# Weight preparation of a two-layer graph kernel in twenty pieces, each with a place of its own in its engine's order

## The chip, the cores and the metric

The kernel runs on one core of a Trainium2 chip. The metric is the device time of one execution in microseconds. The kernel before takes 776.16 us, the median of three runs (776.13 to 776.79). Engines: TensorE (PE, matmul), VectorE (DVE), ScalarE (ACT), GpSimd (POOL) and SyncE (SP, which here only issues DMAs).

## The reference

64 graphs of 128 nodes and 256 features pass through two layers with a residual each.

```python
h = relu(layernorm(x));  x = x + gat(adj, h)      # two graph-attention layers inside
h = relu(layernorm(x));  x = x + mha(h, adj)      # 8 heads of 32, masked
# gat layer 1 (4 heads of 128): xl = h @ W1; a = <xl, att_src>, b = <xl, att_dst> per head
#   attn = softmax over sources of leaky_relu(a + b), masked; out = elu(attn^T xl + b1)
# gat layer 2 (1 head of 256): the same with W2, att_src2, att_dst2, b2, without elu
# mha: softmax(q k^T / sqrt(32)) v, relu, @ Wo
```

## The kernel before, in words

One graph fills the 128 partitions, so the kernel is a loop over 64 graphs. A graph passes through some fifty small functions on five engines. They are software-pipelined: in step t an engine calls each of its functions for graph t minus a lag that stands beside the function in a list (`(gat1_exp, 4)`), in the order of the list. `run` calls a function only while its graph exists; 75 steps in all. Engines synchronise by one semaphore per function; `done` waits for the producer of the same graph, `free` for the reader of the buffer two graphs back, and `after` and `at_ends` (only the first and last 12 graphs) for readers of a PSUM bank that several results share. An engine runs its list strictly in order.

Graph g's way: `norm1_moments`, `variance1` (VectorE), `rsqrt1` (GpSimd), `norm1_apply`, `relu1` (ScalarE), `relu1_low` (VectorE; h is kept as two halves of 16 bits), `norm1_transpose` (a DMA issued by SyncE gives hT), `project1` (TensorE), `ab_high`, `ab_low`, `xl_evac` (VectorE), `transpose_ab`, `abT_copy`, `scores1_mask` and `scores1`, `gat1_leaky`, `gat1_scores` (row maximum), `gat1_exp`, `gat1_recip`, `normalise` (GpSimd), `transpose1`, `gat1_copy` (en), `aggregate1`, `elu_exp` (ScalarE), `elu` (VectorE, h1T), `project2`, `ab2_evac`, `diagonal2`, `scores2`, `gat2_leaky`, `gat2_scores`, `gat2_exp`, `transpose2`, `gat2_copy`, `aggregate2`, `residual1`; the second norm in the same way to h2T; `qk`, `qk_copy`, `qk_low`, `scores3_mask`, `scores3_first`, `scores3_last`, `mha_max` (VectorE: top3, nmx3), `mha_exp_first` and `mha_exp_last` (four exponentials each), `e3_first_halves` and `e3_last_halves` (GpSimd), `e3_transpose_first` and `_last` (DMA), `project_v`, `mha_av`, `att_norm`, `att_copy`, `att_low`, `att_transpose` (DMA), `project_out`, `residual2`, `store`.

Ahead of this the weights are prepared. W1 gets four columns more (`prod`, then sums over each head); its largest element and that of the columns are found, turned and spread over the partitions by TensorE, rounded to powers of two, and the scaled W1 is split into two 16-bit halves. The four projection matrices get the same treatment in one go (`proj_split`: ScalarE's `split_high`, GpSimd's `split_low`). W2 gets two columns from `prod2`, and a product of W2 with ones gives a correction for b2 and for the scores (`shift2`). Before, this stands in blocks that are called in front of a whole step (`before={3: ..., 4: ...}`): VectorE's `prepare_w1`, `prepare_b1` ahead of step 3, `prepare_w2` ahead of step 4; GpSimd's `products_w1` and `picks` ahead of step 3, `products_w2` ahead of 4; TensorE's `spread_largest` ahead of steps 0 and 4; and `w2_sums` inside `project2` and `ab2_evac` of graph 0. SyncE issues x of two graphs, then W1, att1, b1, x, adj, W2, att2, b2 and the projections.

## Time and profile before

| | |
|---|---|
| median of three runs | 776.16 us |
| the profiled execution | 774.69 us |
| its span, first to last instruction | 772.6 us |
| TensorE busy | 716.3 us (93%) |
| VectorE busy | 681.4 us (88%) |
| ScalarE busy | 591.6 us (77%) |
| GpSimd busy | 515.8 us (67%) |

The rows further down come from one profiled execution. Times are us from its first instruction. A window row gives a stretch and its length, then the busy time and, in brackets, the number of instructions of PE, PEld (TensorE's weight loads), DVE, ACT and POOL, the granted TensorE clock, the busy share of the DMA engines and GB/s. A timeline row gives start, duration and the operation with output <- input; "xN" are N instructions merged. Matmul ends are modelled, and consecutive matmuls overlap, so the distance between starts says more than a duration. 32-bit products take two instructions each in the trace.

### The profile page before, as it was taken

How to read it: one execution, taken by the hardware profiler on the slowest of the kernel's cores; microseconds unless marked ns; L12 is line 12 of the kernel's file. 1: busy time of each engine (PE TensorE's matmuls, PEld its weight loads, DVE VectorE, ACT ScalarE, POOL GpSimd, SP SyncE). 2: the span in 40 equal slices, each digit the busy share in tenths (PEclk: the TensorE clock that was granted, in tenths of full speed). 3: DMA queues.
4: the chain of work that ended last, by engine and by line, in shares of the span. 5: the costliest groups of instructions: out<-in, count | busy, mean ns of one | idle time of the engine just before them, and what ended most of it. 6: DMA issues, size and time to landing. Idle time of an engine off the chain costs nothing.

```text
span 772.6 us, 26496 instructions
## 1 busy us (share of the span) xinstructions
PE 716.3 (93%) x8398; PEld 593.4 (77%) x8398; DVE 681.4 (88%) x2017; ACT 591.6 (77%) x1865; POOL 515.8 (67%) x733
## 2 busy tenths in 40 slices
PE   0389999999999999999999999999999999999973
PEld 0157788888888888888888888888888888788852
DVE  4758899999999999999999999999999989999873
ACT  0167888888888778888888788788888888788752
POOL 5456777676767676667667766676677767766551
PEclk9999999999999999999999999999999999999996
DMA  6111555666578566557766656766655666655464
GB/s 197 33 37 43 106 112 112 121 110 118 118 117 115 116 112 113 119 114 115 122 110 118 112 124 115 115 110 120 114 119 116 113 119 106 112 118 105 89 110 89
DMA packets 270423, 84.70 MB, mean 110 GB/s; under 512 B 242896, under 2 KB 269904, under 8 KB 270288
## 3 DMA queue, kind: packets, MB, share of 16 engines
q1 hardware_dynamic: 270288, 83.02, 57.8%
q8 instruction: 70, 1.15, 0.7%
q14 instruction: 65, 0.53, 0.3%
HBM read 15.86 MB, written 8.39 MB: 31 GB/s over the span
## 4 chain that ended last, share of the span: by engine, by line
PE 75%; DVE 9%; DMA 5%; issue 4%; SPq 3%; ACT 1%; POOL 1%; DVEq 0%; ACTq 0%; POOLq 0%
PE bank L815 28%; PE bank L840 11%; PE bank L986 7%; PE bank L947 6%; DMA hT<-h_split 4%; PE bank L966 3%; PE bank L929 3%; PE bank L936 3%; PE bank L866 3%; PE bank L891 2%; PE bank L889 2%; PE bank L881 2%; SPq L276 1%; DVE top L756 1%; PE bank L874 1%
## 5 line engine op out<-in xcount | busy, mean ns | idle before, releaser
L497 ACT ACTIVATE e<-bank,nmx,q_power 128x128 f32<-128x128 f32 x512 | 194.7, 481 | 5.1 <-DVE nmx L761 5.1
L372 POOL CAST e_split<-e 128x512 f16<-128x512 f32 x128 | 82.4, 643 | 118.6 <-ACT e L497 118.6
L374 POOL TENSOR_TENSOR e_split<-e,e_split 128x512 f16<-128x512 f32 x128 | 151.7, 1185 | 10.3
L840 PE MATMUL bank<-w,h1T 128*128 128x258 f32 x512 | 122.8, 382 | 0.7 <-DVE shift L599 0.7
L386 POOL TENSOR_TENSOR rstd<-var,minus_half 128x1 f32<-128x1 f32 x128 | 71.7, 560 | 66.6 <-DVE var L625 66.6
L815 PE MATMUL bank<-w_split,hT 128*128 128x260 f16 x768 | 98.2, 278 | 12.3 <-DMA hT<-h_split 11.9
L840 PEld LDWEIGHTS bank<-w,h1T 128*128 128x128 f32 x512 | 96.6, 190 | 16.6 <-DVE h1T L655 1.6
L448 ACT ACTIVATE eT<-lr,nmx 128x128 f32<-128x128 f32 x256 | 102.7, 458 | 0.8 <-DVE nmx L713 0.8
L815 PE MATMUL bank<-h2T,proj_split 128*128 128x128 f16 x1536 | 97.4, 220 | 1.6 <-DMA h2T<-h_split 1.6
L815 PEld LDWEIGHTS bank<-h2T,proj_split 128*128 128x128 f16 x1536 | 92.0, 99 | 3.7 <-DMA h2T<-h_split 2.4
L815 PEld LDWEIGHTS bank<-w_split,hT 128*128 128x128 f16 x768 | 71.1, 98 | 24.5 <-issue 7.0
L364 POOL TENSOR_TENSOR eTn<-eT,rs 128x512 f32<-128x512 f32 x64 | 67.0, 1046 | 17.9 <-DVE rs L752 17.9
L756 DVE TENSOR_REDUCE top<-bank 128x8 f32<-128x1024 f32 x64 | 77.3, 1208 | 0.3 <-PE bank L947 0.3
L424 ACT ACTIVATE h_split<-z 128x256 f16<-128x256 f32 x64 | 26.6, 416 | 65.9 <-DVE z L631 65.9
L947 PEld LDWEIGHTS bank<-qkT 32*128 32x128 f16 x1536 | 43.0, 93 | 37.7 <-issue 36.0
L986 PE MATMUL bank<-en,xl 128*128 128x128 f32 x512 | 68.3, 276 | 0.2
L448 ACT ACTIVATION_READ_ACCUMULATOR eT<-lr,nmx 128x1 f32 x256 | 65.7, 257 | 0.0
L947 PE MATMUL bank<-qkT 32*128 32x128 f16 x1536 | 64.8, 216 | 0.3 <-DVE qkT L724 0.2
L986 PEld LDWEIGHTS bank<-en,xl 128*128 128x128 f32 x512 | 62.2, 192 | 2.0 <-ACT en L455 1.3
L604 DVE SCALAR_TENSOR_TENSOR h_split<-z,h_split 128x256 f16<-128x256 f32 x128 | 61.5, 481 | 0.6 <-ACT h_split L424 0.5
L815 PE MATMUL bank<-proj_split,attT 128*128 128x256 f16 x384 | 54.3, 279 | 6.1 <-DMA attT<-att_split 6.1
L440 ACT ACTIVATE lr<-bank,ab 128x128 f32<-128x128 f32 x64 | 23.5, 368 | 43.6 <-PE bank L867 43.6
(116 smaller groups left out, 1921.7 us busy)
## 6 DMA issues: line engine op xcount, KB each, us to landing
x_in<-in_x_dram SPq DMA_DIRECT2D x64, 128.0 KB, 2.3
out_dram<-x_out SPq DMA_DIRECT2D x64, 128.0 KB, 2.0
adj_in<-in_adj_dram SPq DMA_DIRECT2D x64, 64.0 KB, 2.5
e3T<-e_split SPq DMA_TRANSPOSE x128, 3.1
hT<-h_split SPq DMA_TRANSPOSE x64, 2.4
h2T<-h_split SPq DMA_TRANSPOSE x64, 2.5
attT<-att_split SPq DMA_TRANSPOSE x64, 2.8
w<-in_L_gnn_W_dram SPq DMA_DIRECT2D x2, 256.0 KB, 3.1
```

What stands on the lines that cost most here:

```text
L364: pool.tensor_tensor(eTn[:, g.two, :].rearrange("p (h n) -> p h n", h=H), eT[:, g.two, :].rearrange("p (h n) -> p h n", h=H), rs[:, g.two, ...
L372: pool.tensor_copy(e3_split[:, g.two, half, 0], e).then_inc(s[high_set], 1)
L374: pool.tensor_tensor(e3_split[:, g.two, half, 1], e, e3_split[:, g.two, half, 0], ALU.subtract).then_inc(s[low_set], 1)
L386: pool.tensor_tensor(rstd[:, g.two, which:which + 1], var[:, g.two, which:which + 1], minus_half[:, :], ALU.pow).then_inc(s[rstd_set], 1)
L448: ins = act.activation(eT[:, g.two, h * N:(h + 1) * N], lr[:, g.two, h * N:(h + 1) * N], ACT.Exp, bias=nmx[:, g.two, h:h + 1], accum_out=s ...
L497: ins = act.activation(e3[:, g.two, h, :], S[:, h // 4, (h % 4) * N:(h % 4 + 1) * N], ACT.Exp, bias=nmx3[:, g.two, h:h + 1], scale=q_power ...
L604: dve.scalar_tensor_tensor(out=out_, in0=in_, scalar=0.0, in1=high_, op0=ALU.max, op1=ALU.subtract).then_inc(s[sem_], 1)
L756: dve.tensor_reduce(top3[:, g.two, :], S.rearrange("p b (h n) -> p (b h) n", h=4), AX.X, ALU.max, negate=True).then_inc(s["top3_set"], 1)
L815: ins = pe.matmul(out_, left, right, start=n == 0, stop=n == len(pairs) - 1)
L840: ins = pe.matmul(X2[:, 0:D + 2], h1T[:, g.two, k * F:(k + 1) * F], w2[:, k, :], start=k == 0, stop=k == H - 1)
L947: ins = pe.matmul(S[:, b, col * N:(col + 1) * N], qkT[r, g.two, i, h // 4, :], qkT[r, g.two, j, 2 + h // 4, :], start=False, stop=n == 2 a ...
L986: ins = pe.matmul(O1[:, h * N:(h + 1) * N], xl[:, g.two, h * F:(h + 1) * F], en[:, g.two, h * N:(h + 1) * N], start=True, stop=True)
```

## The change

Every piece of the preparation becomes a function of its own with a lag in the list of its engine (`@once`: it runs for graph 0 only). The orders and lags of all five engines are written anew, and with them the PSUM banks of the results and the waits `after` and `at_ends`; the arithmetic is the same. A new wait `after_once` guards banks that preparation and loop share. The weights' semaphores are divided (`w1_in`, `att1_in`, `b1_in`; a set of its own for w1 and for proj in place of the counted `power_set` and the like). ScalarE issues the loads of att1 and b1; SyncE issues W1 first.

```diff
-        XL = bank[:, 0:2, :]   ABT = bank[:, 2, ...]   Z = 3   ET = 6   O1 = 1   X2 = 6   Z2 = 7
-        ET2 = 6   O2 = 2   QK = 7   V = 3   S = 4:6   AV = 2   WO = 0
+        XL = bank[:, 6:8, :]   ABT = bank[:, 6, ...]   Z = 2   ET = 0   O1 = 3   X2 = 3   Z2 = 2
+        ET2 = 7   O2 = 6   QK = 7   V = 1   S = 4:6   AV = 0   WO = 0
+        W2_SUMS = bank[:, 4]
+        PREP = {"w1": bank[:, 2], "proj": bank[:, 4]}
...
+def after_once(eng, sem, g, lag, value=1):
+    if 0 <= g.n + lag and g.n < LAGS:
+        eng.wait_ge(sem, value)
...
+        def once(function):
+            def first(g):
+                if g.n == 0:
+                    function(g)
+            return first
...
 SyncE
-            for n in range(2):
-                sp.dma_start(x_in[:, n, :], x[n]).then_inc(x_here[n], 16)
             for k in range(KD):
                 sp.dma_start(w1[:, k, :, 0:HF // 2], ...).then_inc(s["w1_in"], 16)
-            for k in range(2):
-                sp.dma_start(att1[:, k, :], ...).then_inc(s["w1_in"], 16)
-            sp.dma_start(b1_all[:, :], ...).then_inc(s["w1_in"], 16)
-            sp.dma_start(x_in[:, 2, :], x[2]).then_inc(x_here[2], 16)
+            for n in range(3):
+                sp.dma_start(x_in[:, n, :], x[n]).then_inc(x_here[n], 16)
...
-                (e3_transpose_last, 9), (att_transpose, 10), (store, 11), (norm1_transpose, 3), (e3_transpose_first, 8),
-                (load_adj, 1), (load_x, 0), (norm2_transpose, 6),
+                (load_x, 0), (load_adj, 1), (store, 11), (norm1_transpose, 3), (e3_transpose_last, 8), (norm2_transpose, 6),
+                (e3_transpose_first, 8), (att_transpose, 9),
 GpSimd
-                (e3_last_halves, 9), (masks, 3), (e3_first_halves, 8), (rsqrt1, 2), (rsqrt2, 6), (diagonal2, 5),
-                (normalise, 4),
-            before={3: (products_w1(), picks()), 4: products_w2, 5: (split_low(0), split_low(1)), 6: split_low(2), 7: split_low(3)}
+                (products_w2, 4), (e3_first_halves, 11), (e3_last_halves, 10), (split_low3, 11), (rsqrt1, 3), (rsqrt2, 8),
+                (diagonal2, 7), (split_low2, 9), (picks, 1), (products_w1, 1), (normalise, 6), (split_low0, 8),
+                (split_low1, 8), (masks, 3),
 ScalarE
+            for k in range(2):
+                act.dma_start(att1[:, k, :], ...).then_inc(s["att1_in"], 16)
+            act.dma_start(b1_all[:, :], b1.partition_broadcast(128)).then_inc(s["b1_in"], 16)
...
-                (v_copy, 9), (relu1, 3), (gat2_leaky, 6), (att_copy, 10), (abT_copy, 4), (gat1_copy, 5), (gat2_exp, 6),
-                (gat1_leaky, 4), (mha_exp_first, 8), (elu_exp, 5), (gat2_copy, 6), (mha_exp_last, 8), (qk_copy, 7),
-                (gat1_exp, 4), (relu2, 6),
-            before={5: (split_high(0), split_high(1)), 6: split_high(2), 7: split_high(3)}
+                (split_high3, 9), (gat2_exp, 7), (gat1_copy, 6), (att_copy, 11), (v_copy, 9), (gat2_copy, 7), (abT_copy, 5),
+                (mha_exp_last, 9), (elu_exp, 6), (split_high2, 8), (gat1_leaky, 5), (mha_exp_first, 9), (split_high0, 7),
+                (qk_copy, 8), (gat1_exp, 5), (relu1, 3), (relu2, 7), (gat2_leaky, 6), (split_high1, 7),
 VectorE
-                (xl2_evac, 6), (relu2_low, 7), (ab_high, 4), (v_low, 9), (ab_low, 4), (xl_evac, 4), (gat2_scores, 6),
-                (mha_max, 8), (att_low, 10), (relu1_low, 3), (residual2, 11), (norm1_moments, 2), (gat1_scores, 4), (elu, 5),
-                (gat2_recip, 6), (variance1, 2), (residual1, 6), (norm2_moments, 6), (variance2, 6), (qk_low, 7),
-                (ab2_evac, 5), (norm2_apply, 6), (gat1_recip, 4), (att_norm, 9), (norm1_apply, 2),
-            before={3: (prepare_w1(), prepare_b1()), 4: prepare_w2}
+                (w1_largest, 0), (variance2, 7), (v_low, 9), (qk_low, 8), (b1_prep, 4), (ab2_evac, 6), (xl2_evac, 6),
+                (norm2_apply, 7), (proj_row, 6), (w1_sums, 2), (gat1_recip, 5), (norm1_moments, 1), (relu1_low, 3),
+                (att_norm, 10), (relu2_low, 7), (gat2_scores, 6), (ab_high, 4), (xl_evac, 4), (w1_scale, 3), (w1_products, 0),
+                (ab_low, 4), (proj_scale, 6), (w1_row, 2), (mha_max, 8), (gat2_recip, 6), (att_low, 10), (proj_largest, 5),
+                (residual2, 11), (variance1, 1), (residual1, 6), (elu, 5), (norm2_moments, 6), (w2_sums, 4), (w2_shift, 5),
+                (gat1_scores, 4), (norm1_apply, 2),
 TensorE
+            @once
+            def w2_ones(g):
+                pe.wait_ge(s["w2_set"], 2)
+                pe.wait_ge(s["ones_set"], 4)
+                at_ends(pe, s["e3_first"], g, -3)
+                after_once(pe, power_set["proj"], g, -1)
+                for k in range(H):
+                    ins = pe.matmul(W2_SUMS[:, 0:D + 2], ones[:, :], w2[:, k, :], start=k == 0, stop=k == H - 1)
+                ins.then_inc(s["w2_summed"], 1)
...
-                (scores3_mask, 8), (scores3_first, 8), (scores2, 6), (scores3_last, 8), (transpose_ab, 4), (transpose1, 5),
-                (scores1_mask, 4), (scores1, 4), (project_out, 11), (aggregate1, 5), (transpose2, 6), (project_v, 8), (qk, 7),
-                (aggregate2, 6), (project2, 5), (mha_av, 9), (project1, 3),
-            before={0: spread_largest(0, 0, 2, 2), 4: spread_largest(1, 2, 6, 3)}
+                (turn_w1, 0), (spread_w1, 0), (project1, 0), (scores3_last, 4), (transpose1, 1), (project_v, 4),
+                (scores1_mask, 0), (transpose2, 2), (transpose_ab, 0), (project_out, 7), (aggregate1, 1), (aggregate2, 2),
+                (scores1, 0), (qk, 3), (project2, 1), (scores3_mask, 3), (mha_av, 5), (scores3_first, 3), (turn_proj, 1),
+                (scores2, 1), (w2_ones, 0), (spread_proj, 1),
```

## Rows read from the trace of the kernel before

**Rows 1.** Page: busy time of each engine, and the chain by engine.

```profile
PE 716.3 (93%) x8398; PEld 593.4 (77%) x8398; DVE 681.4 (88%) x2017; ACT 591.6 (77%) x1865; POOL 515.8 (67%) x733
...
PE 75%; DVE 9%; DMA 5%; issue 4%; SPq 3%; ACT 1%; POOL 1%; DVEq 0%; ACTq 0%; POOLq 0%
```

**Rows 2.** Windows: busy us (instructions) of each engine, granted clock, DMA.

```profile
0.00:40.00 40.00, 8.63 (x37) 5.12 (x37) 22.64 (x53) 5.55 (x15) 18.40 (x35) 1.00 0.39 111
140.00:640.00 500.00, 496.88 (x5961) 416.93 (x5961) 468.87 (x1411) 415.08 (x1319) 353.29 (x502) 1.00 0.65 116
718.00:773.00 55.00, 38.25 (x483) 29.02 (x481) 32.24 (x81) 28.39 (x84) 21.46 (x27) 0.84 0.52 99
```

**Rows 3.** Timeline of TensorE, `scores1_mask` of six graphs: start, us, what.

```profile
34.31 0.63 PE L881 MATMUL bank<-ident,mask_gat 128*128 128x512 f16 x1
...
61.34 0.38 PE L881 MATMUL bank<-ident,mask_gat 128*128 128x512 f16 x1
...
113.24 0.38 PE L881 MATMUL bank<-ident,mask_gat 128*128 128x512 f16 x1
...
354.97 0.38 PE L881 MATMUL bank<-ident,mask_gat 128*128 128x512 f16 x1
...
365.83 0.38 PE L881 MATMUL bank<-ident,mask_gat 128*128 128x512 f16 x1
...
718.26 0.38 PE L881 MATMUL bank<-ident,mask_gat 128*128 128x512 f16 x1
```

**Rows 4.** Timeline of the head: start, us, what, [idle before, releaser].

```profile
11.06 1.22 DVE L552 TENSOR_REDUCE largest<-w 128x1 f32<-128x1024 f32 x1 [6.18 <-DMA b_all<-in_L_gnn_b_dram]
...
20.83 1.69 DVE L571 SCALAR_TENSOR_TENSOR w_split<-w,scale,w_split 128x512 f16<-128x512 f32 x4
...
24.68 4.64 POOL L345 TENSOR_TENSOR prod<-w,att 128x512 f32<-128x512 f32 x4
...
26.00 2.76 PE L815 MATMUL bank<-w_split,hT 128*128 128x260 f16 x12 [6.99 <-DMA hT<-h_split]
...
45.28 2.01 PE L802 MATMUL bank<-w,ones 128*128 128x258 f32 x8 [1.50 <-DVE h1T L655]
```

**Rows 5.** Timeline of one step in the loop, ScalarE, then VectorE.

```profile
411.46 1.51 ACT L497 ACTIVATE e<-bank,nmx,q_power 128x128 f32<-128x128 f32 x4
...
412.85 0.70 ACT L460 ACTIVATE ex<-bank,minus_one 128x512 f32<-128x512 f32 x1
...
409.86 1.21 DVE L756 TENSOR_REDUCE top<-bank 128x8 f32<-128x1024 f32 x1
...
413.88 0.68 DVE L655 SCALAR_TENSOR_TENSOR h1T<-ex,bank 128x512 f32<-128x512 f32 x1
```

**Rows 6.** Groups of instructions from 200 to 600 us: busy us, mean ns.

```profile
L738 DVE SCALAR_TENSOR_TENSOR x<-bank,rs,x_in 128x256 f32<-128x256 f32 x36 | 17.4, 484 | 12.8 <-PE bank L929 12.8
...
L773 DVE SCALAR_TENSOR_TENSOR x_out<-bank,out_power,x 128x256 f32<-128x256 f32 x37 | 17.4, 472 | 0.0
```

**Rows 7.** The line that applies a norm: duration ns min/median/max.

```profile
L631 DVE TENSOR_SCALAR z<-x_in,mv,rstd x64: 376/798/1256, 4.5 to 704.7; 128x256 f32<-128x256 f32 x64
```

**Rows 8.** SyncE's issue of one hT, its use, the landing of all 64.

```profile
600.24 1.19 SPq L263 DMA_TRANSPOSE hT<-h_split  x1
...
603.41 1.49 PE L815 MATMUL bank<-w_split,hT 128*128 128x260 f16 x12
...
DMA to landing us min/median/max: 2.4/2.4/4.2
```

**Rows 9.** Waits: who waited for whom, us in total, times, longest.

```profile
PE bank L815 <- DMA hT<-h_split: 11.9, 9, 7.0
...
DVE h1T L655 <- ACT ex L460: 8.8, 19, 1.4
```

**Rows 10.** Timeline of the tail: `transpose2` and `qk` of graph 63.

```profile
738.17 0.33 PE L912 MATMUL bank<-ident,eT 128*128 128x128 f32 x1 [0.78 <-ACT eT L471]
...
748.20 2.03 PE L815 MATMUL bank<-h2T,proj_split 128*128 128x128 f16 x18 [1.25 <-DMA h2T<-h_split]
```

More of the change, by code:

```diff
@@ L203, in gnn_kernel @@
         s = {n: sem(n) for n in names}
+        turned = {n: sem(f"turned_{n}") for n in ("w1", "proj")}
+        row_set = {n: sem(f"row_set_{n}") for n in turned}
+        diag_set = {n: sem(f"diag_set_{n}") for n in turned}
+        spread = {n: sem(f"spread_{n}") for n in turned}
+        power_set = {n: sem(f"power_set_{n}") for n in turned}
+        scale_set = {n: sem(f"scale_set_{n}") for n in turned}
         x_here = [sem(f"x_here{i}") for i in range(8)]
@@ L351, in split_low, with split_low0, split_low1, split_low2 @@
                 pool.tensor_tensor(proj_split[:, 1, :, m, :], proj[:, :, m, :], proj_split[:, 0, :, m, :], ALU.subtract).then_inc(s["split_low"], 1)
+            @once
+            def split_low0(g):
+                split_low(0)
+            @once
+            def split_low1(g):
+                split_low(1)
+            @once
+            def split_low2(g):
+                split_low(2)
+            @once
+            def split_low3(g):
+                split_low(3)
             def diagonal2(g):
@@ L549, in prepare_w1, with rows_of_largest @@
-            def prepare_w1():
-                dve.wait_ge(s["w1_in"], 16 * 5)
-                dve.wait_ge(s["ident_set"], 5)
-                dve.tensor_reduce(largest[:, 0:1], w1[:, :, :, high], AX.XYZ, ALU.max, apply_absolute_value=True).then_inc(s["largest_set"], 1)
+            def rows_of_largest(n, first, last):
+                rows, column = last - first, list(turned).index(n)
+                dve.wait_ge(turned[n], 1)
+                dve.tensor_reduce(row_largest[0:rows, column:column + 1], PREP[n][0:rows, 0:128], AX.X, ALU.max).then_inc(row_set[n], 1)
+                dve.wait_ge(row_set[n], 1)
+                dve.tensor_scalar(largest_diag[0:rows, first:last], ident[0:rows, 0:rows], row_largest[0:rows, column:column + 1], None,
+                                  ALU.mult).then_inc(diag_set[n], 1)
@@ L553, in prepare_w1, with w1_largest, w1_products @@
+            @once
+            def w1_largest(g):
+                dve.wait_ge(s["w1_in"], 16 * KD)
+                dve.tensor_reduce(largest[:, 0:1], w1[:, :, :, high], AX.XYZ, ALU.max, apply_absolute_value=True).then_inc(s["largest_w1"], 1)
+            @once
+            def w1_products(g):
+                dve.wait_ge(s["w1_in"], 16 * KD)
+                dve.wait_ge(s["att1_in"], 16 * 2)
                 for k in range(KD):
@@ L785, in _, with turn_w1 @@
         @block.tensor
         def _(pe):
-            def spread_largest(n, first, last, count):
+            @once
+            def turn_w1(g):
                 pe.wait_ge(s["ident_set"], 5)
-                pe.wait_ge(s["ones_set"], 4)
-                pe.wait_ge(s["largest_set"], count)
-                rows = last - first
-                pe.transpose(S[0:rows, n, 0:128], largest[:, first:last], ident[:, :]).then_inc(s["largest_turned"], 1)
-                pe.wait_ge(s["largest_diag_set"], n + 1)
-                pe.matmul(S[:, n, 128:128 + rows], ones[0:rows, :], largest_diag[0:rows, first:last], start=True, stop=True).then_inc(s["largest_spread"], 1)
-                pe.wait_ge(s["power_set"], 2 * n + 1)
@@ L798, in w2_sums, with spread_w1 @@
-            def w2_sums():
+                pe.wait_ge(s["largest_w1"], 2)
+                at_ends(pe, s["lr_set"], g, -1)
+                at_ends(pe, s["lr2_set"], g, -2)
+                pe.transpose(PREP["w1"][0:2, 0:128], largest[:, 0:2], ident[:, :]).then_inc(turned["w1"], 1)
+            @once
+            def spread_w1(g):
+                pe.wait_ge(s["ones_set"], 4)
+                pe.wait_ge(diag_set["w1"], 1)
+                pe.matmul(PREP["w1"][:, 128:130], ones[0:2, :], largest_diag[0:2, 0:2], start=True, stop=True).then_inc(spread["w1"], 1)
@@ new lines, in turn_proj, with spread_proj @@
+            @once
+            def turn_proj(g):
+                pe.wait_ge(s["ident_set"], 5)
+                pe.wait_ge(s["largest_proj"], 1)
+                at_ends(pe, s["e3_first"], g, -2)
+                after_once(pe, s["shift2_set"], g, 0, 2)
+                pe.transpose(PREP["proj"][0:4, 0:128], largest[:, 2:6], ident[:, :]).then_inc(turned["proj"], 1)
+            @once
+            def spread_proj(g):
+                pe.wait_ge(s["ones_set"], 4)
+                pe.wait_ge(diag_set["proj"], 1)
+                pe.matmul(PREP["proj"][:, 128:132], ones[0:4, :], largest_diag[0:4, 2:6], start=True, stop=True).then_inc(spread["proj"], 1)
@@ L799, in w2_sums @@
+            @once
+            def w2_ones(g):
                 pe.wait_ge(s["w2_set"], 2)
                 pe.wait_ge(s["ones_set"], 4)
+                at_ends(pe, s["e3_first"], g, -3)
+                after_once(pe, power_set["proj"], g, -1)
                 for k in range(H):
-                    ins = pe.matmul(X2[:, 0:D + 2], ones[:, :], w2[:, k, :], start=k == 0, stop=k == H - 1)
+                    ins = pe.matmul(W2_SUMS[:, 0:D + 2], ones[:, :], w2[:, k, :], start=k == 0, stop=k == H - 1)
```

193 lines of the change are left out of this document (113 added, 80 removed).

## The prediction

> **What bounds the kernel now.** I read the page's busy times first, then the windows, then the marks of one TensorE instruction per graph, and only then single stretches. The reader is to see that TensorE is busy 93% of the span and that three quarters of the chain that ended last lie on it [rows 1]; that in the middle it is busy 496.88 of 500 us, against 8.63 of the first 40 and 38.25 of the last 55 [rows 2]. So the middle is TensorE's own work, and what can be won cheaply lies in the first 40 us and in the last 55.
>
> The mask product of the first attention (`scores1_mask`) runs once per graph and is my clock for the loop [rows 3]: graph 0 at 34.31, graph 3 at 61.34, graph 8 at 113.24, graph 63 at 718.26. Two neighbours without a disturbance lie 10.86 apart (365.83 - 354.97). From graph 8 to 63 there are 55 steps in 605.0 us, 11.0 each: 55 x 10.86 = 597.3 is TensorE without a gap, 7.7 us are stalls. Three stretches follow: head (to 113.2), loop (605.0) and tail (718.26 to 772.6, 54.3).
>
> **Head.** What the block at the start costs now [rows 4]: VectorE waits until 11.06 for the transfer of b1, the fifth that the first weight semaphore counts; its block runs to 20.83 + 1.69 = 22.5, that is 11.4 us; the first `project1` starts at 26.00, after the halves of h have been made behind the block and turned by DMA. Then the scores of graph 0 and `project1(1)` wait behind the second block, which itself waits for GpSimd's four products (24.68 to 29.3); the first score mask comes only at 34.31 [rows 3]. The sum over W2 on TensorE (2.01 us at 45.28) and its evacuation stand directly ahead of `project2(0)`.
>
> After the change W1 is the first transfer, att1 and b1 are issued by ScalarE, and b1 is waited for only in its own piece. The gate of the W1 products is then att1's landing. The bounds are 4.9 (where VectorE fell idle, 11.06 - 6.18) and 11.06; two loads of x no longer stand ahead and b1 is no longer counted, but W1 and att1 are 1 MB that still have to come, so I take 8.0. The rest of the W1 block is 11.4 - 1.2 (the maximum, done while att1 lands) = 10.2 us, and between its pieces now stand three moments of x, one norm and one remainder, some 2.3 us by the loop's durations: the W1 pieces end at 20.5. hT is issued some 3 us before that and takes 2.4 to land [rows 8], so it is covered. `project1(0)` starts at 20.5, 5.5 earlier.
> Rule against it, which none of these numbers uses: the Trainium skill, DMA: Bandwidth & Descriptors, section Issuing engines are not separate DMA queues, says that transfers from any engine share the same DMA engines and that a second issuer saves only issue time. By that ScalarE's three issues save some 1.5 us and the rest must come from the order; the sum would be about 2 us later. No row of this kernel shows loads issued by ScalarE.
>
> From there I followed graph 0 by the durations of the trace. xl is done at 23.2 (2.76 us for the product [rows 4]), ab_split 24.3, scores 26.0, leaky 26.8; VectorE does the W2 sums (2.4 us) just in that wait, so they are nearly free; row maximum 27.5, exponentials 29.2. `w2_ones` takes 2.0 us of TensorE ahead of `project1(1)`; it ends near 28.9, `project1(1)` near 31.5, mask of graph 1 at 32. `proj_largest` (2.3 us) falls into the wait for graph 0's transpose, normalised copy and aggregation, so `project2(0)` starts near 35.8 (now some 48, behind the W2 sums). Then: mask of graph 2 near 41, of graph 3 near 50 (now 61.34). Here the price of the split pieces falls due: eight ScalarE copies of 512 elements (0.7 us as `elu_exp` [rows 5]) and four GpSimd subtractions (1.2 us, a quarter of its four products) sit in steps in which graphs 1 to 3 already run; I give them 1.2 us in all, graph 4 at 60.7. Then TensorE is full: 9.6 + 10.2 + 10.2 + 10.9 (the step without, with `mha_av`, with `project_out`) and 0.8 for stalls puts graph 8 at 102.4. Head: 113.2 - 102.4 = **10.8 us won**. Bounds: 13 (dense from graph 3 on) and 5 (the split pieces and the W2 pieces each hold a whole step up, as the second block does now).
>
> **Loop.** The instructions are the same, but the diff rewrites every engine's order, the PSUM banks and the waits between engines; so "no change" has to be shown. I laid the new orders out against TensorE's dense 10.86 us, with zero at `project1`. TensorE's hand-overs fit: ab_split is ready at 2.4, wanted at 3.1; en at 3.0, wanted by `project_out` at 3.25 (its bank is ET's); h1T at 6.8, wanted at 7.1; diag2 at 9.7, wanted at 10.4; the score bank free at 7.8, wanted at 8.8. Two circles are tight.
> Circle one goes `mha_max` -> four exponentials -> `elu_exp` -> `elu` -> VectorE's order -> next `mha_max`. ScalarE's part is 1.4 us to the start of `elu_exp` (411.46 to 412.85) + 0.70 + hand-overs, 2.2 in all [rows 5]. In the order of before five pieces of VectorE fill that gap; now it holds att_low, two residuals [rows 6] and two ops of 0.15, 1.3 us by issue spacing. So VectorE idles 0.9 us there. Its busy time is 468.87 / 500 x 11.0 = 10.31 us a step [rows 2], and 10.31 + 0.9 = 11.2 would be over 10.86. But of this 10.31 the norm of x takes 0.80 (median; shortest 0.38 [rows 7]), with GpSimd at work beside it; in the new order it falls where GpSimd has finished the late halves and waits for variance2. With 0.4 instead of 0.8, and 0.2 of overlap of the small ops' tails (issued 0.07 to 0.09 apart, 0.15 long), the circle is 10.6 to 10.8: just under TensorE.
> Circle two goes over SyncE. In the order of before hT is issued at 600.24 and used at 603.41 [rows 8], 3.2 us on; it lands in 2.4 (up to 4.2), and hT's lateness makes 4.9 of the 7.7 us of stalls (11.9 less the 7.0 of the first [rows 9]). Now `store` and `norm1_transpose` stand behind `e3_transpose_first` and `att_transpose` and two loads. By my layout e3_transpose_first is issued at 4.3, and 1.25 + 1.25 + 0.5 + 0.6 + 0.6 us of issues later hT at 8.5, for a use at 10.86: 2.36 us for a landing of 2.4. That circle spans two steps and gives 10.95 us a step, and it has no room for a slow landing. 55 x 10.95 = 602.3 and 1.7 for slow ones: 604, **1 us won**. Both ends: 597.3 (-7.7) and 11.15 a step, 613 (+8).
>
> **Tail.** After graph 63's mask the rest of a graph's chain runs alone. Now `transpose2(63)` is at 738.17, and `qk(63)` at 748.20 [rows 10], 10.0 us on; in the new order `aggregate2` stands ahead of `qk(62)`, not behind it (1.5 us), and `transpose2(63)` comes some 0.8 us earlier from the mask. The rest (two e3 transposes, `mha_av`, out, store) keeps its length. **2.3 us won**, bounds 0 and 4.
>
> **Sum.** The profiled execution took 774.69 (span 772.6 and 2.1 around it). 774.69 - 10.8 - 1.0 - 2.3 = 760.6. The median of the runs is 776.16, 1.5 above the profiled one: 762.
>
> **Rivals.** A, the loop gets denser: hT lands in time after all and both circles stay under 10.86: 762 - 6 = 756. For it: GpSimd's late halves could be earlier than I placed them; against it the 2.36 us.
> B, VectorE becomes the bound through circle one: the norm keeps 0.80 because GpSimd works beside it. 11.1 us a step, 55 x 0.15 = 8 us over my 10.95: 770. For it: `elu` already waited 19 times, 8.8 us, for `elu_exp` [rows 9]. Beside this, the Trainium skill, SBUF — State Buffer, section Who interferes with whom: a VectorE operation in a two-port mode and GpSimd lock each other out for a whole instruction; the 376 to 1256 ns of one shape [rows 7] agree that it can be long, though the median is twice the shortest and not a whole GpSimd instruction of 1.2 us more.
> C, the pieces hold the first graphs up: head won only 5 us: 768.
> D, slower than before: SyncE's queue sets the loop. If the issue of hT comes 0.6 us later than placed (att_low behind GpSimd's halves, a store that waits for `project_out`) the two-step circle is 22.5 us, 11.25 a step, 55 x 0.3 = 16 us over my loop: 778. It decides against the change from 0.27 us a step over 10.95 on, where 55 x 0.27 eats the 14 us.
> E, a loop stall that cancels the head: 775 to 778.
>
> **How the numbers follow.** Chances: forecast 0.52, A 0.14, B 0.14, C 0.08, D 0.09, E 0.03. The forecast with A, B and C makes faster, 0.88, less a little for B and C falling together: 0.85. No change (within 0.2%, 1.6 us, about what a measurement tells) is E and the edge of D: 0.04. Slower: 0.11. The range has the low end at 762 less the rest of A and 2 us of head (753), the high end at B with 5 us of C (775).
>
> **What would show it.** Right: masks of graph 0 near 24, graph 3 near 50, graph 8 near 102; `project2(0)` near 36; norm of x (L631's line) well under 0.8; VectorE idle at `elu` in most steps but TensorE without gaps; hT issued 2.3 to 2.5 us before `project1`. Wrong: att1 landing after 9.5; mask distances over 11.1 in the middle; a wait of TensorE for h1T or hT in every step (B or D); a gap over 2 us at `qk(0)` or `project_v(0)` for the split weights (C).

## The result, and the profile after

The changed kernel takes 812.42 us (median of 4 runs, 809.96 to 817.27) against 776.14 us (775.66 to 776.79), a ratio of 1.0475, interval 1.0423 to 1.0526. It is 36 us slower; the forecast was 762 us, and even rival D, the one on the slower side, gave 778.

The profiled execution took 817.27 us, its span is 814.8; it is the slowest of the four, so stretches read from it are some 5 us longer in sum than the median's. I read it in the order in which the prediction was made. First the page, busy times and the chain by engine, which answers to [rows 1]:

```profile
PE 729.6 (90%) x8398; PEld 598.9 (74%) x8398; DVE 682.6 (84%) x2017; ACT 586.8 (72%) x1865; POOL 532.0 (65%) x733
...
ACT 23%; issue 18%; DVE 13%; PE 13%; DMA 11%; SPq 11%; POOL 10%; POOLq 0%; ACTq 0%; DVEq 0%
```

The reader is to see the second line. No engine's busy time has grown by more than 17 us, but the chain that ended last has left TensorE: 75% of it was there, now 13%, and the rest wanders over every engine and over SyncE's queue (SPq). That is what a kernel looks like that is bound by a circle of waits and not by an engine. The windows, columns as in [rows 2]:

```profile
0.00:40.00 40.00, 13.97 (x64) 9.46 (x65) 26.30 (x61) 7.17 (x18) 24.54 (x43) 1.00 0.45 125
140.00:640.00 500.00, 473.34 (x5528) 392.93 (x5526) 434.49 (x1311) 382.12 (x1227) 339.74 (x465) 0.99 0.61 108
762.00:815.00 53.00, 36.35 (x477) 27.63 (x474) 32.06 (x80) 28.16 (x82) 21.15 (x26) 0.85 0.55 101
```

The head is fuller (13.97 us of TensorE in 40, not 8.63), the middle has lost what made it dense: 473.34 of 500 and not 496.88. `scores1_mask` (L997 now), to be laid beside [rows 3]:

```profile
26.27 0.63 PE L997 MATMUL bank<-ident,mask_gat 128*128 128x512 f16 x1
...
54.07 0.38 PE L997 MATMUL bank<-ident,mask_gat 128*128 128x512 f16 x1
...
113.38 0.38 PE L997 MATMUL bank<-ident,mask_gat 128*128 128x512 f16 x1
...
762.07 0.38 PE L997 MATMUL bank<-ident,mask_gat 128*128 128x512 f16 x1
```

| stretch | before | predicted | after |
|---|---|---|---|
| head, to the mask of graph 8 | 113.2 | 102.4 | 113.4 |
| loop, graph 8 to 63 | 605.0 (11.00 a step) | 604 (10.95) | 648.7 (11.79) |
| tail | 54.3 | 52.0 | 52.7 |

The whole loss is the loop's 43.7 us. The head's gain was there (8.0 us at graph 0, 7.3 at graph 3) and was given back by graph 8. A part of that is the new, slower loop, in which those five steps already run: e11, below, has the loop mended and takes 56.0 us from graph 3 to graph 8, against 59.3 here and 51.9 before. In the waits (who waited for whom, us in total, times, longest) two things that hardly showed before now lead at TensorE:

```profile
PE bank L927 <- DMA hT<-h_split: 28.7, 24, 2.3
...
DVE h1T L748 <- ACT ex L517: 24.7, 37, 1.5
...
PE bank L953 <- DVE h1T L748: 10.4, 26, 1.1
```

Inside the loop (marks 8 to 63) they make 27.0 us for hT (23 times) and 6.0 for h1T (20 times), against 3.3 for hT before. That is 29.7 of the 43.7. The rest is busy time: 473.34/500 x 11.79 is 11.16 us of TensorE a step against 10.93 before, 12.6 us over 55 steps. Some 3.2 of them are three `project1` that ran wholly or partly at the lower clock (2.78, 2.78 and 2.10 us instead of 1.49, see below). That the others are matmuls that start after a gap and so don't overlap with a neighbour (42 gaps in the middle 500 us, 11 before) is my reading and not shown.

The chain of waits between 301 and 325 us says why hT is late; start, us, what:

```profile
305.94 1.44 ACT eT L505 x7
...
308.93 0.71 POOL absent L437
...
309.72 0.95 POOL mask_mha L438
...
310.73 0.46 POOL mask_gat L440
311.19 0.56 POOL e_split L408
...
311.83 1.17 POOL e_split L410
...
313.01 1.23 SPq L278
...
314.34 1.25 SPq L297
...
315.64 0.57 SPq L263
...
316.26 0.42 SPq L269
316.73 0.43 SPq L273
...
317.25 4.63 DMA hT<-h_split
...
321.93 2.78 PE bank L927 x12
```

This is circle two of the prediction with its full length. GpSimd makes the masks (2.3 us with their gaps, 308.93 to 311.19) and only then the halves of e3; SyncE issues the turn of e3 (L278), then that of att (L297), two loads and the store, and hT last: 317.25, some 4.2 us behind the e3 issue, though h was ready long before (in a later step its remainder is made at 416.39 and the turn issued at 425.32). `project1` starts the next round through the queues: `transpose1` stands behind it on TensorE (L1085, from 325.23), ScalarE's `gat1_copy` waits for that near the head of its list, and the exponentials of the mha and of the first attention stand behind `gat1_copy` and feed the same GpSimd queue. The wait of `gat1_copy`, over the whole kernel:

```profile
ACT en L512 <- PE bank L1085: 41.5, 32, 3.5
```

From `ex` at 303.07 to `ex` two steps on, at 328.65, the same chain takes 25.6 us; 2.2 of it are a slow landing (4.63 instead of the median 2.4). Without it, 23.4/2 = 11.7 a step. This slow landing costs twice: TensorE had stood for 2.0 us, and its 12 matmuls took 2.78 us and not 1.49. The window of just that product shows the lower of the two clock levels, 0.50 (1.2 GHz):

```profile
321.90:324.70 2.80, 2.77 (x14) 1.71 (x16) 0.00 (x0) 0.46 (x2) 2.42 (x4) 0.50 0.31 61
```

One more view, a step on VectorE and GpSimd side by side (timeline, columns as in [rows 5]). It is where the second surprise lies:

```profile
416.39 0.93 DVE L697 SCALAR_TENSOR_TENSOR h_split<-z,h_split 128x256 f16<-128x256 f32 x1
...
417.82 0.42 DVE L697 SCALAR_TENSOR_TENSOR h_split<-z,h_split 128x256 f16<-128x256 f32 x1
...
420.40 0.70 DVE L852 TENSOR_SCALAR nmx<-top,q_power 128x8 f32<-128x8 f32 x1
```

```profile
416.00 1.04 POOL L400 TENSOR_TENSOR eTn<-eT,rs 128x512 f32<-128x512 f32 x1 [0.54 <-DVE rs L843]
...
417.80 0.95 POOL L438 TENSOR_SCALAR mask_mha<-adj_in 128x128 bf16<-128x128 int32 x1
...
419.91 1.16 POOL L410 TENSOR_TENSOR e_split<-e,e_split 128x512 f16<-128x512 f32 x1
```

The two remainders have one line and one shape. That of h, `relu1_low`, starts inside GpSimd's `normalise` and takes 0.93 us; that of h2, `relu2_low`, takes 0.42, though GpSimd is at work there too, on `mask_mha`, and it is `mask_mha` that takes 0.95 where it took 0.66 elsewhere. The scaling of nmx3, 8 columns, takes 0.70 when it meets the subtraction of the halves, and ends 0.03 us behind it (421.10, 421.07); in the step before, with GpSimd idle, it took 0.23 (409.22). By this the Trainium skill, SBUF — State Buffer, section Who interferes with whom, is borne out in kind: VectorE and GpSimd share a pair of ports and lock each other out.

### The profile page after: what moved, and what is told of

Read it like the earlier page. It is cut to its first block, busy times and chain, and to the rows that moved or that the text cites. A ratio compares the mean times of both kernels' runs of the same rounds, so it can differ in the third digit from the quotient of the medians.

```text
span 814.8 us, 26593 instructions
## 1 busy us (share of the span) xinstructions
PE 729.6 (90%) x8398; PEld 598.9 (74%) x8398; DVE 682.6 (84%) x2017; ACT 586.8 (72%) x1865; POOL 532.0 (65%) x733
## 4 chain that ended last, share of the span: by engine, by line
ACT 23%; issue 18%; DVE 13%; PE 13%; DMA 11%; SPq 11%; POOL 10%; POOLq 0%; ACTq 0%; DVEq 0%
ACT e L554 11%; DMA hT<-h_split 9%; ACT eT L505 7%; PE bank L927 6%; SPq L297 4%; SPq L278 3%; POOL e_split L410 3%; DVE top L847 3%; ACT ex L517 2%; POOL mask_mha L438 2%; POOL absent L437 2%; PE bank L1085 2%; DVE nmx L852 2%; SPq L263 2%; POOL e_split L408 2%
## 5 line engine op out<-in xcount | busy, mean ns | idle before, releaser
L408 POOL CAST e_split<-e 128x512 f16<-128x512 f32 x128 | 78.9, 616 | 133.7 <-ACT e L554 133.7
L953 PE MATMUL bank<-w,h1T 128*128 128x258 f32 x512 | 126.3, 389 | 11.0 <-DVE h1T L748 10.4
L953 PEld LDWEIGHTS bank<-w,h1T 128*128 128x128 f32 x512 | 92.1, 190 | 26.8 <-DVE h1T L748 15.6
L505 ACT ACTIVATE eT<-lr,nmx 128x128 f32<-128x128 f32 x256 | 101.5, 438 | 2.3 <-DVE nmx L804 2.3
L528 ACT ACTIVATE eT<-lr,nmx 128x128 f32<-128x128 f32 x64 | 25.7, 402 | 92.0 <-DVE nmx L796 92.0
L927 PEld LDWEIGHTS bank<-h2T,proj_split 128*128 128x128 f16 x1536 | 88.2, 98 | 3.4 <-DMA h2T<-h_split 3.3
L697 DVE SCALAR_TENSOR_TENSOR h_split<-z,h_split 128x256 f16<-128x256 f32 x128 | 90.4, 708 | 0.3
L512 ACT ACTIVATE en<-bank 128x512 f32<-128x512 f32 x64 | 38.1, 595 | 42.9 <-PE bank L1085 41.5
L748 DVE SCALAR_TENSOR_TENSOR h1T<-ex,bank 128x512 f32<-128x512 f32 x64 | 44.0, 687 | 25.3 <-ACT ex L517 24.7
L505 ACT ACTIVATION_READ_ACCUMULATOR eT<-lr,nmx 128x1 f32 x256 | 60.6, 237 | 0.0
L438 POOL TENSOR_SCALAR mask_mha<-adj_in 128x128 bf16<-128x128 int32 x64 | 55.3, 864 | 5.1
```

Of the source, the lines that this page charges most:

```text
L408: pool.tensor_copy(e3_split[:, g.two, half, 0], e).then_inc(s[high_set], 1)
L438: pool.tensor_scalar(mask_mha[:, g.eight, :], adj_in[:, g.four, :], 0.0, -BIG, ALU.is_equal, ALU.mult)
L505: ins = act.activation(eT[:, g.two, h * N:(h + 1) * N], lr[:, g.two, h * N:(h + 1) * N], ACT.Exp, bias=nmx[:, g.two, h:h + 1], accum_out=s ...
L697: dve.scalar_tensor_tensor(out=out_, in0=in_, scalar=0.0, in1=high_, op0=ALU.max, op1=ALU.subtract).then_inc(s[sem_], 1)
L927: ins = pe.matmul(out_, left, right, start=n == 0, stop=n == len(pairs) - 1)
L953: ins = pe.matmul(X2[:, 0:D + 2], h1T[:, g.two, k * F:(k + 1) * F], w2[:, k, :], start=k == 0, stop=k == H - 1)
```

## Experiments

Two theories stood at the start. **SyncE's queue** (rival D, circle two): hT waits behind e3, att, loads and store. **VectorE and ScalarE** (circle one): from the row maximum `mha_max` over ScalarE's exponentials and back through VectorE's order. Each edit is against the changed kernel unless said otherwise; "step" is the loop's us per graph between the marks of graphs 8 and 63, read from one execution. The kernel before was measured again beside each group of runs (medians 776.14, 773.74, 772.65 and 773.15 us), so kernels of different groups are compared by their ratios.

| kernel | us | ratio to before, 95% | step |
|---|---|---|---|
| changed kernel | 812.42 | 1.0475 (1.0423 to 1.0526) | 11.79 |
| e1, hT ahead on SyncE | 792.02 | 1.0223 (1.018 to 1.0266) | 11.38 |
| e2, moments moved | 819.88 | 1.0586 (1.0538 to 1.0635) | 11.80 |
| e3, both | 794.58 | 1.0265 (1.0226 to 1.0304) | 11.36 |
| e5, pieces in the old loop | 769.77 | 0.9957 (0.9935 to 0.9979) | 11.01 |
| e4, masks between the halves | 780.17 | 1.0093 (1.0066 to 1.012) | 11.18 |
| e6, other places | 787.96 | 1.0194 (1.015 to 1.0238) | 11.33 |
| e7, `elu_exp` first | 819.60 | 1.06 (1.055 to 1.0651) | 11.87 |
| e9, W2 pieces later | 774.31 | 0.9998 (0.9969 to 1.0026) | 11.03 |
| e10 = e4 + e1 | 770.66 | 0.9966 (0.995 to 0.9981) | 11.03 |
| e11 = e10 + a swap | 767.08 | 0.9916 (0.9884 to 0.9947) | 10.96 |

**e1, hT ahead on SyncE.** The turn of h is issued one step earlier, behind the last half of e3, and no longer at the end of the queue.

```diff
 SyncE
-    (load_x, 0), (load_adj, 1), (store, 11), (norm1_transpose, 3), (e3_transpose_last, 8), (norm2_transpose, 6),
+    (load_x, 0), (load_adj, 1), (store, 11), (e3_transpose_last, 8), (norm1_transpose, 2), (norm2_transpose, 6),
```

> The changed kernel with one edit on SyncE: norm1_transpose stands ahead of norm2_transpose with lag 2 instead of behind store with lag 3, so hT is issued some 8 us ahead of its use. In the changed kernel the loop from graph 8 to 63 took 648.7 us (11.8 a step); project1 waited for hT 28.7 us in 24 of its steps, and project2 for h1T 10.4 us. Theory 1 (a circle over two steps, project1 -> VectorE -> GpSimd's normalise, masks and first halves -> SyncE's queue -> hT -> project1, sets the loop; the circle mha_max -> exponentials -> elu_exp -> elu comes second): no wait for hT is left, the second circle then gives about 11.3 a step, loop 620, total 784. Theory 2 (the circle through elu sets the loop, the wait for hT only follows from it): the waits move to h1T, loop stays above 640, total 805 or more. Theory 3 (either alone explains all): loop 600, total 764.

Measured: 20 us faster than the changed kernel; every wait for hT is gone (in the loop `project1` now starts 10.2 to 10.9 us after the issue), and the step is 11.38. Theory 1 had 11.3 and 784 us: the right case, 8 us too low. What is left is the other circle:

```profile
DVE h1T L748 <- ACT ex L517: 41.5, 59, 1.5
...
PE bank L953 <- DVE h1T L748: 15.2, 36, 1.1
```

So SyncE's queue sets the step at 11.79, and a second circle lies close below it, at 11.38. Taking the first away gives only half of the loss back.

**e2 and e3, the moments of x moved.** `norm1_moments` goes out of the crowded part of VectorE's order into the gap in which `elu` waits: alone (e2), and with e1's edit (e3).

```diff
 VectorE
-    (gat1_recip, 5), (norm1_moments, 1), (relu1_low, 3),
+    (gat1_recip, 5), (relu1_low, 3),
...
-    (residual2, 11), (variance1, 1), (residual1, 6), (elu, 5),
+    (residual2, 11), (norm1_moments, 1), (variance1, 1), (residual1, 6), (elu, 5),
```

> The changed kernel with one edit on VectorE: norm1_moments moves from behind gat1_recip to just ahead of variance1, that is into the gap between mha_max and elu, where VectorE waits for ScalarE. That takes 0.55 us out of the circle mha_max -> exponentials -> elu_exp -> elu and nothing out of the circle over SyncE. Theory 1: the wait for hT stays, the loop gains 0 to 0.2 us a step, total 801 to 812. Theory 2: 0.5 us a step, total 785.

> Both edits together. Theory 1: both circles come near TensorE's own 10.9 us: 10.9 to 11.1 a step, loop 600 to 610, total 765 to 775, and more is gained than by the two edits singly. Theory 2: as the second edit alone, 785. A third theory (VectorE's longer remainders and nmx3 beside GpSimd are a cost in themselves, whatever the circles): above 780, with VectorE busy over 95%.

Measured: e2 gained nothing in the loop (11.80), as it must while SyncE's queue sets the step. In all it is even slower than the changed kernel (1.0586 against 1.0475, the intervals apart) and above both of its expectations; why is open, since the two profiled executions differ by 1.1 us only. But e3 gained nothing over e1 either (11.36 against 11.38), and 0.6 us had been taken out of what I held to be the circle. Its time lies with the third theory, above 780, but VectorE is busy 90% and not over 95%, so none of the three was met. The chain of e3 between two row maxima shows both what the circle really is and where the 0.6 us went:

```profile
407.51 1.14 DVE top L847
...
408.68 0.71 DVE nmx L852
...
410.92 0.11 ACT ex L517
...
411.37 0.71 ACT lr L490
412.08 0.63 ACT e L554 x2
...
413.79 1.69 ACT eT L505 x8
415.48 0.32 ACT h_split L481
...
415.82 0.07 DVE h_split L697
415.89 1.13 issue
417.02 0.21 DVE rs L785
...
419.00 1.14 DVE top L847
```

The circle doesn't return through `elu`. It goes on along ScalarE's queue, over leaky, the other four exponentials (`mha_exp_first`) and the four of the first attention (`eT`, 413.79), and enters VectorE again behind them: 11.49 us from maximum to maximum. In e1 it takes the same way, except that it enters VectorE at `norm1_moments`, which stands behind `gat1_recip` and its wait for `eT`; between 200 and 600 us the chain of e1 passes `mha_max` 34 times and `elu` once. And the 0.6 us are eaten at one place. With the moments gone the remainder starts together with GpSimd's `normalise` and takes 1.27 us, not 0.93; ahead of it VectorE waits for ScalarE's relu. In e1 and in e3 `rs` (L785) starts at the same 417.02. Over the whole kernel the mean of the two remainders is 871 ns in e3 and 859 in e2, against 708 in the changed kernel and 481 before.

**e5, the pieces in the old loop.** The kernel before, with its own lists, banks and lags, and only the preparation cut up and the load order changed. ScalarE's split copies, GpSimd's products and subtractions and the first W1 pieces of VectorE and TensorE still stand in blocks ahead of whole steps; in the changed kernel all 27 pieces (not twenty, as the title has it) have places of their own.

```diff
 SyncE: W1 first; att1 and b1 issued by ScalarE
 GpSimd
+    before={2: products_w1, 3: picks, 4: products_w2, 6: (split_low(0), split_low(1)), 7: split_low(2), 8: split_low(3)}
 ScalarE
+    before={6: (split_high(0), split_high(1)), 7: split_high(2), 8: split_high(3)}
 VectorE (once each, for graph 0; the other entries as before)
+    before={2: (w1_largest, w1_products), 3: w1_sums}
+    (b1_prep, 4), (w2_sums, 4), (w1_row, 3), (w1_scale, 3), (proj_largest, 4), (w2_shift, 5), (proj_row, 5), (proj_scale, 5),
 TensorE
+    before={0: (turn_w1, spread_w1)}
+    (w2_ones, 4) behind scores1; turn_proj, spread_proj (5) behind project2
```

> The kernel before with its loop orders, lags and banks kept as they are, and only the preparation cut into pieces between the first graphs (and W1 loaded first, att1 and b1 issued by ScalarE). If the head is worth what the changed kernel's head showed at graph 0 to 3 (marks 8.0 and 7.2 us earlier), and the loss is all in the loop, this gives 766 to 769. If the pieces cost as much in the first eight steps as they give, as the changed kernel's mark of graph 8 (113.4 against 113.2) could also be read, it stays at 775 to 777.

Measured: 4 us faster than before, between the two cases (the first meant 7 to 10), and the loop is the old one (11.01). So this cutting up is worth 0.4%, and the 36 us are all in the rewritten orders with their lags and banks. Of 8.8 us at graph 0 (25.52 against 34.31) 4.8 are left at graph 8: GpSimd's `products_w2` hold the W2 sums to 28.4, and `w2_ones`, 3.81 us of TensorE from 30.76, stands ahead of `project1(1)`.

**e4, masks between the halves.** GpSimd makes the masks of a graph between the two sets of halves, as before the change, not ahead of both.

```diff
 GpSimd
-    (products_w2, 4), (e3_first_halves, 11), (e3_last_halves, 10), ...
-    (split_low1, 8), (masks, 3),
+    (products_w2, 4), (e3_first_halves, 11), (masks, 4), (e3_last_halves, 10), ...
+    (split_low1, 8),
```

> The changed kernel with one edit on GpSimd: masks (2.2 us) stand between e3_first_halves and e3_last_halves (lag 4), where GpSimd waits 1.6 to 2.8 us for the exponentials, and no longer between normalise and e3_first_halves. SyncE's order stays. Theory 1 (the two-step circle runs through normalise, masks, first halves and SyncE's queue): e3T, and with it hT, is issued up to 2 us earlier, the wait of project1 for hT all but goes, and the time falls as with hT issued early, to 788 to 796. If the circle does not run through GpSimd: 808 to 816.

Measured: one function moved, and by the ratios some 29 of the 36 us are back (step 11.18), more than the 788 to 796 us expected. It cuts both circles. The e3 issue ahead of hT comes 14.2 us after the `project1` of two graphs earlier, not 15.9 (means of graphs 12 to 61); and nmx3 no longer meets the subtraction. The page's group for nmx3, and what is left of the waits:

```profile
L852 DVE TENSOR_SCALAR nmx<-top,q_power 128x8 f32<-128x8 f32 x64 | 15.5, 241 | 2.3
```

```profile
PE bank L927 <- DMA hT<-h_split: 9.0, 10, 1.2
```

241 ns and not 467, 0.23 us in each turn of circle one.

**e6, other places.** SyncE issues hT behind the first half of e3 (still ahead of att), and the remainder of h goes away from `normalise`, behind `residual2`.

```diff
 SyncE
-    (store, 11), (norm1_transpose, 3), (e3_transpose_last, 8), (norm2_transpose, 6), (e3_transpose_first, 8), (att_transpose, 9),
+    (store, 11), (e3_transpose_last, 8), (norm2_transpose, 6), (e3_transpose_first, 8), (norm1_transpose, 2), (att_transpose, 9),
 VectorE
-    (norm1_moments, 1), (relu1_low, 3), ... (residual2, 11), (variance1, 1),
+    (norm1_moments, 1), ... (residual2, 11), (relu1_low, 3), (variance1, 1),
```

> The changed kernel with hT out of the way of SyncE's queue (norm1_transpose with lag 2 behind e3_transpose_first) and relu1_low moved into the gap between mha_max and elu, behind residual2, where GpSimd waits for exponentials. With moments alone in the gap VectorE's wait at elu fell but relu1_low, now starting with normalise, took 1.27 us instead of 0.41 and the step stayed 11.36. Theory (circle through elu, lengthened by VectorE's operations with two SBUF inputs beside GpSimd): 0.9 us leave the circle, the loop is TensorE's 10.9 to 11.0 a step, total 764 to 772. Rival (the loop is bound by something else that all of these share, such as VectorE's amount of work): 11.2 or more a step, 785 or more.

Measured: step 11.33, 787.96 us. The mean of the remainders fell to 489 ns, so the length is a matter of the neighbour. But the test of the sum is spoilt: the new place on SyncE holds the loads back, a new wait that I had not counted:

```profile
DVE stats L710 <- DMA x_in<-in_x_dram: 38.1, 34, 3.1
...
POOL absent L437 <- DMA adj_in<-in_adj_dram: 23.3, 27, 2.9
```

Inconclusive for circle one.

**e7, `elu_exp` first.** e1's edit, and ScalarE makes `elu_exp` ahead of the four last exponentials.

```diff
 ScalarE
-    (mha_exp_last, 9), (elu_exp, 6), (split_high2, 8), (gat1_leaky, 5), (mha_exp_first, 9),
+    (elu_exp, 6), (mha_exp_last, 9), (split_high2, 8), (gat1_leaky, 5), (mha_exp_first, 9),
```

> The changed kernel with hT issued early (as in the first experiment) and on ScalarE elu_exp ahead of mha_exp_last. That cuts the circle mha_max -> exponentials -> elu_exp -> elu at ScalarE and leaves VectorE's order and its slow remainders as they are. Circle theory: the wait of project2 for h1T (15 us) goes, 10.9 to 11.1 a step, 765 to 775. Rival (VectorE's amount of work beside GpSimd): stays at 785 to 792.

Measured: the waits of VectorE for `ex` go, and the step gets longer, 11.87. ScalarE now stands at the head of its queue for TensorE's aggregation in every graph, with all exponentials behind it:

```profile
ACT ex L517 <- PE bank L1105: 66.8, 64, 1.3
```

My expectation failed: taking the wait of `elu` away shortened no circle. Nor is it a clean test of the way through `elu`, for the norm of x is back at a mean of 819 ns (425 in e1). Whether ScalarE's standing alone makes the 11.87 was not separated.

**e9, W2 pieces later.** e5 with `w2_sums` behind `gat1_scores`, `w2_ones` behind `aggregate1` of graph 0, GpSimd's `products_w2` one step earlier and `proj_largest` at the head of VectorE's list.

```diff
 GpSimd (of e5)
-    before={..., 3: picks, 4: products_w2, ...}
+    before={..., 3: (products_w2, picks), ...}
 VectorE (of e5)
-    (xl_evac, 4), (w2_sums, 4), (gat2_scores, 6), ... (gat1_scores, 4), (proj_largest, 4), (elu, 5),
+    (proj_largest, 5), ... (xl_evac, 4), (gat2_scores, 6), ... (gat1_scores, 4), (w2_sums, 4), (elu, 5),
 TensorE
-    (scores1, 4), (w2_ones, 4), (project_out, 11), (aggregate1, 5),
+    (scores1, 4), (project_out, 11), (aggregate1, 5), (w2_ones, 5),
```

> The old loop with the pieces, and the W2 pieces placed anew: GpSimd's W2 products earlier, the W2 sums behind the first row maximum, the product with ones behind aggregate1(0), where TensorE waits, and the maximum of the projections in front of project1(1)'s evacuation. In the first version the product with ones took 3.8 us directly ahead of project1(1), and the mark of graph 1 came 11.5 us behind that of graph 0 (7.5 in the kernel before). If that is what ate the head's gain: mark of graph 8 at 104 to 106 (now 108.4), total 766 to 768. If not, 770.

Measured: the mask of graph 0 at 28.35 (25.52 in e5), of graph 8 at 112.5 (108.4); no gain over before is left. The expectation missed: the places of the pieces in e5 were better than mine. Which piece cost the 4 us was not separated.

**e10 and e11.** e4's and e1's edits together, and then VectorE's `att_norm` ahead of `relu1_low`, so that the remainder starts later than `normalise`.

```diff
 VectorE (e11 only)
-    (relu1_low, 3), (att_norm, 10), (relu2_low, 7),
+    (att_norm, 10), (relu1_low, 3), (relu2_low, 7),
```

> The changed kernel with both single edits that worked: masks between the two halves on GpSimd, and hT issued early on SyncE (norm1_transpose, lag 2, ahead of norm2_transpose). With masks alone the loop took 11.18 a step: 11.0 in most steps, 0.1 of it a wait for h1T, and up to 1.5 in some for hT (11.9 in all). If what is left of the two-step circle is those waits for hT: 11.0 a step, loop 605, total 768 to 772. If moving masks already broke the circle and the rest is landing jitter that any order meets: 778 to 782.

> The kernel of e10 with att_norm ahead of relu1_low on VectorE, so that relu1_low (two SBUF inputs) starts when GpSimd's normalise is done. relu1_low took 0.95 beside normalise and takes 0.41 alone. If it is held up by normalise and lies on the circle through elu: 0.45 us off that circle, the last 0.1 us a step of wait for h1T goes, 10.9 a step, 3 to 6 us less than e10, total 763 to 767. If relu1_low is slow for another reason it stays at 0.9 and the time stays within 1 us of e10.

Measured: e10 770.66 us, e11 767.08, both against 773.15 for the kernel before in the same sitting. In e10's chain the circle from maximum to maximum is 11.00 us (406.12 to 417.12): 11.49 less the 0.47 that nmx3 lost. In time both expectations came out (e10 768 to 772; e11 3 to 6 us less than e10), with the circle named wrongly as the one through `elu`. In e11 it falls below TensorE's own work, most steps are 10.90, and the page's chain is back on TensorE. The 0.45 us are not all won, though: `relu1_low` takes 0.41, but `relu2_low` now 0.83 (0.41 in e10), and the mean of both fell from 701 to 665 ns only. How the last gain of 3.6 us comes about is therefore not shown:

```profile
140.00:640.00 500.00, 497.57 (x5967) 422.03 (x5968) 460.75 (x1415) 412.81 (x1323) 360.99 (x502) 1.00 0.64 116
```

```profile
PE 69%; DVE 10%; ACT 9%; issue 6%; DMA 4%; SPq 1%; POOL 0%; POOLq 0%; DVEq 0%; ACTq 0%
```

TensorE is busy 497.57 of 500, as much as before the change (496.88). e11 beats both kernels: the rewritten orders with three entries elsewhere are 0.8% (0.5 to 1.2) faster than the kernel before and 5.3% faster (767.08/773.15 against 1.0475) than the kernel as changed.

## Why the prediction was wrong, by its own steps

The profiled executions give 817.27 - 774.69 = +42.6, predicted -14.1. The 56.7 between them are the loop, 44.7, the head, 11.0, the tail, 0.7, and 0.4 around the span.

**Loop: the step that failed is the size of circle two.** The prediction wrote "That circle spans two steps and gives 10.95 us a step", with a landing of 2.4 and room for no slower. The mechanism was right, and rival D named it; the price was not. Measured it is 11.79 a step. Laid out by the terms of that sum, as means over graphs 12 to 61 and from one `project1` to the one two graphs on:

| part of circle two | reckoned | measured |
|---|---|---|
| `project1` to the issue of e3's first half | 10.86 + 4.3 = 15.2 | 15.9 |
| from there to the issue of hT | 4.2 | 4.65 |
| from there to its use | 2.36 | 3.2 |
| two steps | 21.7 | 23.7 |

The largest miss is the last: the landing, put at 2.4 with 1.7 us in the whole loop for slow ones, has the median 2.4 but the mean 2.92, since 18 of these 50 landings take over 2.6 us (8 before, 7 in e1). In a circle without room each of them comes in at full length, three of them with a `project1` wholly or partly at the lower clock on top. What makes them slow is open. The first part hangs on GpSimd's queue: of the 0.7 us some 0.4 are two operations of the masks lengthened beside VectorE (means 0.71 and 0.90 us, 0.54 and 0.66 before), and all of the masks' 2.3 us stand ahead of the halves. e4 shows what that place costs: the masks moved, the step fell by 0.61 us. D's own size, 11.25 a step, was still 0.5 short: its 0.6 us for a late e3 issue was right, but it left the other two parts as they were. A smaller misreading stands beside this: the 4.9 us of stalls that I gave to hT in the loop of before were not all the loop's; between the marks of graphs 8 and 63 it is 3.3.

**Loop: circle one was drawn wrong.** I closed it through `elu_exp` and `elu` at 10.6 to 10.8 us. The chains of e1, e3 and e10 close it through ScalarE's `gat1_exp`, 11.0 to 11.5 us, and pass `elu` hardly ever; e10, with 0.47 us less in nmx3, is 0.49 us shorter from maximum to maximum, as this circle asks. Its length I had built from VectorE's busy time of before with one correction, the norm of x from 0.80 to 0.40. That correction was right (425 ns in the mean, 775 before; 606 to 406 for the second norm). But the collisions with GpSimd had only moved:

```profile
L697 DVE SCALAR_TENSOR_TENSOR h_split<-z,h_split 128x256 f16<-128x256 f32 x128 | 90.4, 708 | 0.3
```

```profile
L852 DVE TENSOR_SCALAR nmx<-top,q_power 128x8 f32<-128x8 f32 x64 | 29.9, 467 | 2.3
```

Per step the norms lost 0.35 + 0.20 and the remainders and nmx3 gained 2 x 0.23 + 0.17: nothing won. Rival B had the collision but on the wrong instruction, and 8 us for it; the circle that it meant costs, by e1, 11.38 - 10.95 = 0.43 a step, 24 us. It was hidden behind the worse one.

**Head: right in kind, 4 us short at graph 3, and then the loop.** `project1(0)` started at 23.70, not 20.5:

```profile
8.55 1.22 DVE L614 TENSOR_REDUCE largest<-w 128x1 f32<-128x1024 f32 x1 [8.55 <-DMA w<-in_L_gnn_W_dram]
...
16.34 1.19 DVE L598 TENSOR_SCALAR largest_diag<-ident,row_largest 2x2 f32<-2x2 f32 x1
...
17.51 1.32 DVE L724 TENSOR_SCALAR z<-x_in,mv,rstd 128x256 f32<-128x256 f32 x1
```

I had the maximum done while att1 lands, and the products from 8.0; W1 itself was there at 8.55 and the maximum came first, so the products began at 9.69. Each of W1's two transfers took 6.2 us to land (median), 3.1 before, with ScalarE's three loads issued at 0.78 to 1.67 beside them. With that the trace agrees with the rule that I had set against myself (the Trainium skill, DMA: Bandwidth & Descriptors, section Issuing engines are not separate DMA queues): the loads of a second issuer interleave with those of the first. No run tells their part from that of the three loads of x issued right behind W1. Then two VectorE operations beside GpSimd's products of 4.69 us took 1.19 us (for 2x2 elements, 0.22 before) and 1.32 (0.40 elsewhere). `w2_ones` took 3.81 us, not 2.0, its products 0.64 us each and not 0.38, while the record gives a clock of 1.00; why is open. And `project2(0)` came at 39.49, not 36. Graph 3 was at 54.07, predicted 50. From there to graph 8 I had reckoned 52.4 us of dense TensorE and it took 59.3: circles one and two again. e11 has the same head and the loop mended, and reaches graph 8 at 108.8: 6.4 of the 11.0 us missing there are the head's own, 2.8 up to graph 3 (52.76), 1.1 from there to graph 4 (11.83, reckoned 10.7), 2.5 up to graph 8. I had given the split pieces 1.2 us in these steps. They are hardly the cause: four ScalarE copies ran and not the eight that I had counted, and e5, with the same pieces in blocks in the old orders, takes 51.9 us from graph 3 to graph 8, as the kernel before does. So it is more likely something in how the new orders start up; what, no run shows.

**Tail: right.** 52.7 us after the last mask, 52.0 predicted. `transpose2(63)` comes 19.5 us behind the mask (19.9 before) and `qk(63)` 28.9 (29.9).

What was to show it wrong did: distances over 11.1 in the middle and waits for hT and h1T, if in 23 and 20 of the 55 steps and not in every one. The chance of 0.11 for slower was too small for a diff that rewrites five orders at once with two circles reckoned at 0.0 to 0.3 us from the bound.

## What to carry to other kernels

In a software-pipelined loop every engine's queue is part of the dependency graph: follow a late result round through the queues until the chain comes back to itself, and charge the circle with all that stands ahead in each queue, with mean and not median landings, and with collisions. A circle reckoned within a few per cent of the bound is a coin toss, and five orders rewritten at once hide the second circle behind the first; change one order at a time. If a good change of the head comes with a new loop, measure it in the old loop first (e5), for then the loss has a name.
